# A decoder attention with two feed-forward layers on one core: other rows for the query stack, an earlier warm-up, and another order of TensorE's work

## The reference

```python
x = x + _layernorm(_L0_attn_ref(_layernorm(x), Wqkv, Wo))     # x: 2 x 1024 x 512
x = x + _layernorm(_L0_ffn_ref(_layernorm(x), ...))           # 4-bit weights, 512 -> 1376 -> 512, silu gate
x = x + _layernorm(_L1_attn_ref(_layernorm(x), mask, weight, bias))   # block-masked 512 x 512 product
x = x + _layernorm(_L1_ffn_ref(_layernorm(x), ...))           # 512 x 512 product and a Fourier update
```

```python
qkv = hidden_states @ Wqkv
q = qkv[..., :nH * d].reshape(B, S, nH, d)
k = qkv[..., nH * d:nH * d + d]
v = qkv[..., nH * d + d:]
scores = jnp.einsum('bqhd,bkd->bhqk', q, k) * scale
scores = jnp.where(causal, scores + slopes * (pos_k - pos_q), NEG_INF)
probs = jax.nn.softmax(scores, axis=-1)
attn = jnp.einsum('bhqk,bkd->bqhd', probs, v).reshape(B, S, H)
return attn @ Wo
```

## Time and profile before

| | us |
|---|---|
| median of 3 runs | 1184.68 |
| profiled execution, its own time | 1178.79 |
| its span | 1177.1 |
| TensorE busy | 1108.0 (94%) |
| VectorE busy | 721.5 (61%) |
| ScalarE busy | 623.6 (53%) |
| GpSimd busy | 420.3 (36%) |

### The profile page before, as it was taken

The page is one execution under the profiler, slowest core; times in us unless marked ns, Lnnn a source line. Parts: engine busy times, 40 slices in busy tenths (PEclk is TensorE's granted clock), DMA queues, the critical chain, the costliest instruction groups (busy, mean ns, idle before and its releaser), DMA issues.

```text
span 1177.1 us, 16357 instructions
## 1 busy us (share of the span) xinstructions
PE 1108.0 (94%) x5888; PEld 673.6 (57%) x5888; DVE 721.5 (61%) x1676; ACT 623.6 (53%) x1067; POOL 420.3 (36%) x493
## 2 busy tenths in 40 slices
PE   6689989999999999999998889999999999999997
PEld 5444533543533433334433567788878878777885
DVE  6588599699689998999812455242132142237674
ACT  4266737586768779898686344311111111126775
POOL 4247325225221083243156555321121111123765
PEclk9899999999999999999999999999999999999999
DMA  5912600400340311122221122330020023202001
GB/s 150 183 17 87 123 19 27 110 19 2 86 68 19 100 28 39 44 64 47 30 90 36 54 60 62 114 108 1 1 87 22 1 52 125 72 36 72 37 36 72
DMA packets 70957, 70.62 MB, mean 60 GB/s; under 512 B 39854, under 2 KB 45510, under 8 KB 70852
## 3 DMA queue, kind: packets, MB, share of 16 engines
q1 hardware_dynamic: 67148, 59.82, 19.8%
q0 software_dynamic: 3152, 8.63, 2.4%
q10 hardware_dynamic: 576, 1.11, 0.3%
HBM read 50.27 MB, written 18.87 MB: 59 GB/s over the span
## 4 chain that ended last, share of the span: by engine, by line
PE 71%; DVE 18%; ACT 3%; DMA 3%; issue 2%; POOL 1%; SPq 1%; POOLq 0%; DVEq 0%; ACTq 0%
DVE bank L1195 8%; PE PO L1502 8%; PE ST L1488 7%; PE f_pair L61 7%; PE f_pair L63 7%; PE f_pair L62 7%; PE bank L1404 6%; DVE mx L1197 4%; PE f_Y L1896 3%; PE f_Y L1898 3%; PE f_Y L1897 3%; PE l_psum L2321 2%; PE l_psum L2323 2%; PE l_psum L2322 2%; PE bank L1474 1%
## 5 line engine op out<-in xcount | busy, mean ns | idle before, releaser
L1107 ACT ACTIVATE PT<-ST,lowered 128x512 f32<-128x512 f32 x576 | 357.2, 690 | 84.7 <-PE ST L1488 55.6
L1195 DVE CUSTOM_DVE_ANT_0 bank<-bank,tail_mask 128x512 f32<-128x512 f32 x320 | 211.6, 719 | 22.8 <-PE bank L1404 22.4
L1404 PE MATMUL bank<-KS,QS 125*128 125x512 bf16 (+2 forms) x896 | 206.3, 311 | 18.0 <-DMA QS<-q_scratch 5.8
L1488 PE MATMUL ST<-QS,KS 128*128 128x512 bf16 x576 | 195.8, 383 | 8.6 <-DMA QS<-mparts 5.2
L1197 DVE TENSOR_REDUCE mx<-bank 128x2 f32<-128x512 f32 (+2 forms) x256 | 160.9, 679 | 29.5 <-PE bank L1407 16.6
L1404 PEld LDWEIGHTS bank<-KS,QS 125*128 125x128 bf16 x896 | 76.0, 99 | 137.3 <-DVE mx L1195 40.6
L1502 PE MATMUL PO<-PT,V 128*32 128x512 f32 x1152 | 152.6, 604 | 0.5 <-ACT PT L1107 0.5
L1822 DVE TENSOR_TENSOR f_h<-f_h,f_pair 128x512 f32<-128x512 f32 (+1 forms) x44 | 30.2, 686 | 197.1 <-ACT f_h L1766 197.1
L1025 POOL TENSOR_SCALAR_AFFINE_SELECT PT<-PT 128x512 f32<-128x512 f32 x128 | 78.3, 640 | 188.5 <-ACT PT L1107 188.3
L1766 ACT ACTIVATE f_h<-f_pair 128x512 f32<-128x512 f32 (+1 forms) x44 | 26.3, 598 | 217.2 <-PE f_pair L63 217.2
L1726 POOL TENSOR_TENSOR f_h_part<-f_h,f_h_part 128x512 fp32r<-128x512 f32 (+1 forms) x44 | 56.8, 1292 | 233.7 <-ACT f_h_part L1770 233.7
(11 more groups left out here) (210 smaller groups left out, 1769.0 us busy)
## 6 DMA issues: line engine op xcount, KB each, us to landing
QS<-q_scratch SPq DMA_DIRECT2D x96, 128.0 KB
q_scratch<-QP SPq DMA_DIRECT2D x36, 128.0 KB, 1.9
xres<-_attn_hidden_states_dram POOLq DMA_DIRECT2D x16, 256.0 KB, 3.1
x_dram<-xout POOLq DMA_DIRECT2D x16, 256.0 KB, 2.4
xin<-x_dram SPq DMA_DIRECT2D x4, 1024.0 KB, 6.8
f_xsum<-x_dram SPq DMA_DIRECT2D x4, 1024.0 KB, 6.8
x_dram<-f_xsum SPq DMA_DIRECT2D x4, 1024.0 KB, 4.6
out_dram<-l_xout SPq DMA_DIRECT2D x7, 512.0 KB, 2.8
```

The source lines that it names most:

```text
L1107: act.activation(PT[:, quad % PT_RING, n % 4, :], ST[:, n % ST_RING, :], ACT.Exp, bias=lowered[:, 0:1]).then_inc(p_done, 1)
L1195: v.tensor_tensor_reduce(at(u), at(u), tail_mask[:, :], 1.0, -3e38, ALU.add, ALU.max, mx[:, i % 2, z, h:h + 1]).then_inc(bank_free_dve, 1)
L1404: last = pe.matmul(at(u)[:, j * w:(j + 1) * w], QS[0:ROWS1, slot, h + j, :], KS[b][0:ROWS1, k0:k0 + w], start=(j == 0 or not diag), stop=( ...
L1488: pe.matmul(ST[:, n % ST_RING, :], KS[b][0:ROWS2, kb * P:(kb + 1) * P], QS[0:ROWS2, slot, h:h + 4, :], start=True, stop=True).then_inc(st_ ...
```

## The change

1. Rows six apart. Set `g` of the stack stands in rows g, g+6, g+12 and so on, where before it stood in 16 neighbouring rows. `q_scratch` has the four column groups inside a dimension, so a transfer has 16 rows of 8 KB and not 64 of 2 KB. The order of the heads inside a block, the key weights, the masks and the position rows follow.
2. The start. TensorE's warm-up products no longer wait for the constants. The slots' position rows are all loaded before the first queries are written. The first block's loads of part 0 are issued ahead of the last write of piece 0. GpSimd takes the low part of the weights' first group, ahead of the reciprocal deviation; VectorE no longer does. ScalarE takes the fourth group's high part before it copies the transposes.
3. The load of piece 2 is issued behind the maxima rows of block 1, and not with the transpose of block 0's maxima.
4. The planner. A projection unit is due 1000 before TensorE's time (500 behind it before), a finish unit 1200 behind (600). Work that will become ready in the next 300 no longer counts as load. A stack is taken to be there after 4500 and not 6500, and 3000 behind the one before.

The core of the diff:

```diff
-            end["stacked", i] = max(t + 6500, end.get(("stacked", i - 1), 0) + 6000)
-            free["sp"] = t + 600
+            end["stacked", i] = max(t + 4500, end.get(("stacked", i - 1), 0) + 3000)
+            free["sp"] = t + 1500
...
-        dve_load = free["dve"] + sum(690 for j, r in pend["dve"] if r <= free["pe"] + 300)
-        act_load = free["act"] + sum(600 for j, r in pend["act"] if r <= free["pe"] + 300)
+        dve_load = free["dve"] + sum(690 for j, r in pend["dve"] if r <= free["pe"])
+        act_load = free["act"] + sum(600 for j, r in pend["act"] if r <= free["pe"])
...
-        for work, late in ((finish_work, 600), (chunk_work, 500)):
+        for work, late in ((finish_work, 1200), (chunk_work, -1000)):
...
-            if u == ("mt", 0):
-                sp_issue(("load", 2), e)
...
                 sp_issue(("mdma", j[1]), done)
+                if j[1] == 1:
+                    sp_issue(("load", 2), done)
...
-        q_scratch = nc.dram_tensor("q_scratch", (B, QB, PARTS, 4, HD, P // HD, P), BF16).ap()
+        q_scratch = nc.dram_tensor("q_scratch", (B, QB, PARTS, HD, P // HD, 4, P), BF16).ap()
...
+            def stack_part(i, part):
+                (b, qb), slot = BLOCKS[i], i % QSLOTS
+                sp.wait_ge(q_out[part], Q_OUT * (piece_of(i) + 1))
+                for g in range(SETS):
+                    if Q_PART[g] == part:
+                        sp.dma_start(QS[g:SETS * HD:SETS, slot, :, :].rearrange("d h q -> d (h q)"),
+                                     q_scratch[b, qb, part].rearrange("d h m q -> d (h m q)")).then_inc(qs_in[slot], 16)
...
-                for g, part in enumerate(Q_PART):
-                    sp.wait_ge(q_out[part], Q_OUT * (piece_of(i) + 1))
-                    sp.dma_start(QS[g * HD:(g + 1) * HD, slot, :, :].rearrange("d (m h) q -> d m (h q)", m=4),
-                                 q_scratch[b, qb, part].rearrange("m d h q -> d m (h q)")).then_inc(qs_in[slot], 16)
+                for part in range(PARTS):
+                    stack_part(i, part)
...
-                if slot == 0:
-                    for m, part in ((0, 0), (1, 0), (0, 1), (0, 2), (2, 0), (1, 1), (1, 2), (3, 0), (2, 1), (2, 2), (3, 1), (3, 2)):
-                        q_part_out(0, m, part)
-                    stack(0)
+            for m, part in ((0, 0), (1, 0), (0, 1), (0, 2), (2, 0), (1, 1), (1, 2), (3, 0), (2, 1), (2, 2), (3, 1)):
+                q_part_out(0, m, part)
+            stack_part(0, 0)
+            q_part_out(0, 3, 2)
+            stack_part(0, 1)
+            stack_part(0, 2)
...
+            weights_low(0)
             piece_rstd(0)
...
+            weights_high(3)
             copy_out(("xt", 0, 0))
             copy_out(("xt", 0, 1))
-            weights_high(3)
...
-            pe.wait_ge(consts_in, 32)
...
             for _ in range(WARM_UP):
                 pe.matmul(PO[:, 0:2 * P], zeros[:, 0:P], zeros[:, 0:2 * P], start=True, stop=True)
+            pe.wait_ge(consts_in, 32)
```

34 lines of the change are left out of this document (17 added, 17 removed).

## The result

| | before | after |
|---|---|---|
| median of the runs, us | 1183.23 (1178.47 to 1185.53, 4 runs) | 1153.58 (1149.85 to 1155.38, 4 runs) |
| profiled execution / its span | 1178.79 / 1177.1 | 1155.38 / 1153.6 |

The ratio is 0.9747 (0.9717 to 0.9777): 29.6 us less, against 19.8 forecast. The two profiled executions lie at opposite ends of their series (before near its fastest, after its slowest), so the traces have to explain 23.5 and not 29.6. Runs of one kernel differ together with TensorE's mean granted clock: of the four runs of after, the one at 0.992 has a span of 1148.1, those at 0.987 have 1151.5 and 1152.2, the profiled one at 0.986 has 1153.6.

What follows compares the result with a forecast made beforehand. TensorE, 94% busy, was taken as the bound, with gains only in the attention: start 9.7, middle 6.2, stall 0.7, tail 3.2, together 19.8 off 1184.68, giving 1165 us. Forecast's own range 1155 to 1175, outer range 1147 to 1182.

Steps and rivals of the forecast that it cites:

- Start: Up to the first score tile: warm-up, stack and second load together take 9.7 us less, bounds 4.5 and 13.1.
- warm-up: Start: warm-up products no longer wait for the constants; first query remainder and everything behind it come 4.5 us earlier.
- stack: Start: the first stack's loads in the new shape, rows six partitions apart, take 3.1 us less.
- six transfers: The stack's six loads in the new shape take 5.5 us, where they took 8.6; bounds 4.6 and 8.1.
- second load: Start: the 1 MB load moved behind block 1's rows of maxima takes 2.1 us off the wait before the first tile.
- Middle: Stretch 160 to 200 us: score tiles now go between the maxima, so TensorE's idle 6.2 us goes.
- stall: TensorE's wait for stack 15 at 576.50, 0.65 us: it goes, counted as 0.7 less.
- tail: End of the attention: block 14's finish fills waits around the last value products, 3.2 us less, bounds 0 and 4.
- (a): Rival, chance 0.18: the middle tightens further, most of 19.5 us idle goes and the tail gains its bound; 1151.
- (b): Rival, chance 0.12: VectorE bounds all through, so the start's gain is absorbed and only the tail is left; 1182.
- (c): Rival, chance 0.10: a piece's projections in one run stop exponentials for 16.4 us; all 30 lost give 1195.
- (d): Rival, counted within the forecast's 0.60: the stack's new shape does nothing or is slower, its 3.1 stays; 1168.

Runs made afterwards that it cites:

- old rules: The changed kernel with the planner's four edits undone, start, stack layout and load place kept; median 1170.14 us, ratio to before 0.9898.
- order alone: The kernel before with the planner's four edits and nothing else; median 1169.43 us, ratio to before 0.9899.
- early load: The changed kernel with the second 1 MB load at its old place in SyncE's order; median 1156.33 us, ratio to before 0.9782.
- experiment 1: The same run as old rules: the changed kernel with the planner's four edits undone; median 1170.14 us.
- old layout: The changed kernel with queries' scratch and stack rows as before (16 neighbouring rows, 64 pieces of 2 KB); median 1158.65 us, ratio to before 0.9803.
- experiment 3: The same run as old layout: the changed kernel with the stack in 16 neighbouring rows again; median 1158.65 us.

## Why the prediction was right, and where its size was off

**The bound** was named rightly: nothing in the last 457 us moved, all of it came from the attention.

**Start, forecast 9.7.** The edits of the start are worth 12 in both pairs of traces (old rules against before 12.0, after against order alone 11.8). Term by term: warm-up 4.5, measured 3.5 at the first query product, 1.4 at the first maxima, and 5.3 to 5.9 in the runs; stack 3.1, measured 2.9 from the first issue to the first maxima; six transfers 5.5, measured 5.98 with nothing between them and 7.0 to 8.0 with the last write between; second load 2.1, measured 2.4 at the rows' landing, 0.5 at the first value product. What I set to nothing was the order's part in the start: I followed it only from the first tile on. By the two pairs of traces it costs 5.9 to 6.1, of which only some 3 are left at like clock; it goes through GpSimd's queue, as the chain shows. So the start as a whole gained 5.9. The first maxima missed their mark by 3 with either order (33.46, and 33.17 with the old rules): 1.1 in the first load's issue (26.15, not 25.1) and 1.8 in what followed (7.3, not 5.5). The first tile missed its mark by 3 through the order and the clock: with the old rules it is at 50.63, where I had 51.5. That the interleaved write "adds nothing" is neither shown nor refuted. I had named Wo's low part as what the last write waits for, and kept "the old distances" to it; they were not kept. The moved load, which I called tight, stalled nothing: its statistics stand at 71.83 with no wait.

By the ports that a transfer reaches (the Trainium skill, SBUF — State Buffer, Door 1: The DMA port swizzle) the stack would have been bound by its issue, 4.6 by the old rows. The issue of six itself now takes 3.67 (early load) where it took 2.65, and the load 5.98; the direction of the rule holds, its gain over my 5.5 does not show.

**Middle, forecast 6.2, stall 0.7, tail 3.2: 10.1 behind the first tile.** Measured 17.5 (after) and 17.3 (order alone). This is the term that was mis-sized. I read 6.2 as the idle time of 160 to 200 and 19.5 as the idle time of all 13 stretches, and so as the bound. But idle time is what stands between two *latencies*; a product that waits for its bank loses 0.17 more inside "busy". By the length of the run less its work, up to 11.8 was to be had there instead of 6. The other 5.5 of the 17.3 are not placed, and experiment 1, without the run and no shorter, says that the gain is that of the new order as a whole. Of the tail's 3.2, the idle rows show 1.1: before 6.1, and after 5.0 (2.09 ahead of the last transposes, 1.46, 1.09, 0.39 in small ones). The wait for stack 15 is gone, as forecast.

**The rivals.** (a) came nearest: 1151 for a middle that tightens all through. The middle did tighten all through, but not as it said: of the idle time behind the first value product, 27.8, only 8.3 went, and the rest came out of "busy". That its sum fits is luck, since the start and the tail gave less than it has. (b), the start's gain absorbed: not so, a start 11.8 later at the same order (order alone) ends 11.9 later, and one 3.7 later (old layout) ends 3.4 later. (c), the projections in one run: it happens, with no exponential from 79.2 to 106.6 in after, longer than the 16.4 that I had counted, and costs nothing that the sum shows; ScalarE is busy for 12.28 of the 13.4 us behind it, but only 15.97 and 14.12 of 20 in the next two stretches, so it catches up. The kernel with the rule undone is 6.4 slower. (d) falls with experiment 3.

**Where 29.6 come from, when the traces have 23.5:** from the draw of the profiled runs. That of before is 4.4 below its median (1178.79 against 1183.23), that of after 1.8 above (1155.38 against 1153.58). At like clock the early warm-up is in the medians and not in the traces. The forecast stood against 1184.68; against 1183.23, the median with the fourth run, its 19.8 make 1163.4.

## What to carry to other kernels

Size a stretch of TensorE by its length less the pipelined time of its work (count times 0.22 for 512 columns here), not by its idle time: products that wait one by one hide part of the loss in busy time (0.17 of 0.43 here). Do not size it by the busy time of a group, which depends on what stands beside it. When a planner's rules change, follow the new order on every queue from the first instruction on, above all what one long operation of a side engine now stands ahead of. Judge such rules together and on the chip: three of them, each undone alone, cost 24 us where all four together cost 16.6. And look at the plan that comes out: one moved load was enough to give another order under the same old rules, so undoing the rules was not undoing the order. Read a difference of a few microseconds in one trace beside the granted clock of the same stretch.

## What the hardware showed that was not expected

- An earlier warm-up can lose its gain again: with 0.88 and 2.82 idle behind it the clock was at 1.2 GHz for the first 5.3 us of query products; warmed up 6 us later and with 1.57 idle, the first product ran at full clock.
- A low part of the weights on VectorE takes 1.09 alone and 2.41 while GpSimd does one (9.30 to 11.10), in the first row:

```profile
9.63 2.41 DVE L1336 TENSOR_TENSOR wx<-PT,wx 128x512 fp32r<-128x512 f32 x1
...
13.17 1.09 DVE L1336 TENSOR_TENSOR wx<-PT,wx 128x512 fp32r<-128x512 f32 x1
```

  The Trainium skill (SBUF — State Buffer, Who interferes with whom) says that a VectorE instruction with two inputs there and a GpSimd instruction that reads it exclude each other; both are such, and the trace agrees.
- Transfers of 16 rows of 8 KB, six partitions apart, take longer to issue than those of 64 pieces of 2 KB: 3.67 for six (early load, at 46.01) against 2.65.
